# An attention and mixture-of-experts block: an own order for the last four batches, padding written during the steps, and expert rows turned by the transfer that loads them

## The chip, the cores and the metric

The kernel runs on one core of a Trainium2 chip. The metric is the time of one execution on the device, in microseconds (us). The core has a TensorE (PE, with its weight loads PEld), a VectorE (DVE), a ScalarE (ACT), a GpSimd (POOL), a SyncE (SP) that here only issues transfers, and 16 DMA engines that all queues share. TensorE runs at one of two clock levels, 1.2 and 2.4 GHz, shown as 0.5 and 1.0.

## The reference

Sixteen batches of 256 tokens of width 128 go through a block of two halves: causal linear attention with 16 heads, and a top-2 mixture of 8 experts. Each half is scaled, shifted and gated by vectors made from a condition `c`.

```python
h = layernorm(x) * (1 + ca) + sa
x = x + ga * attn(h)            # relu features, cumulative k v^T, num / den, out_w
h = layernorm(x) * (1 + cb) + sb
# ffn: 4096 tokens
u = h @ W_in.T;  h = rmsnorm(u, in_norm_w);  logits = h @ Wr.T
idx = top_k(logits + expert_bias, 2);  gates = softmax(logits[idx])
for e in range(8):
    oe = rmsnorm((silu(h @ Wg[e].T) * (h @ Wu[e].T)) @ Wd[e].T, enorm_w[e])
    out += gates[:, e] * oe
x = x + gb * (rmsnorm(out, out_norm_w) @ W_out.T)
```

## The kernel before

**Stage 1, the steps.** A batch passes through six stages of a software pipeline: `nrm` (first norm), `qkv`, `att` (running products of the attention), `prj` (division, output projection, second norm), `inp` (input projection of the experts, sum of squares) and `rte` (routing: best two experts, places, scatter of the rows). `pipelined` calls `step(nrm, qkv, att, prj, inp, rte)` on every engine with the batches s, s-1, ... s-5. Steps 0 to 7 are written out, steps 8 to 15 run in a loop, and steps 16 to 20 are written out again. In the last four of these, step 17 holds batch 15 in `att`, 14 in `prj`, 13 in `inp` and 12 in `rte`, and each later step has one stage fewer. Within a step every engine has one fixed order, written for a full step.

Routing of a batch b: ACT writes the high fp16 half of each row into `rows` (L595, L598); DVE then makes logits (L898), scores (L904), the low fp16 half (L952), the best two (L912, L919), their one-hot (L925); PE turns these into ranks (L1458 to L1464); DVE makes the places `pos` (L931, L947) and the counts (L938). POOL waits for `pos` and sends four indirect transfers of 128 rows of 516 B each (L524) into `hbuf` ("dispatched"), a DRAM buffer with a region of 4352 rows for each expert.

**Between the stages.** When batch 15 is counted, DVE makes `tail` (L1113, L1114), the end of each expert's rows, and SP and ACT write one padding tile of 256 rows (129 KB) behind each of the eight ends (L414, L717). DVE then makes the table of tiles (L1117 to L1136), the gates' logit differences (L1138 to L1143), and the low half of the down weights (L1148); ACT makes the high half (L703; chunks 0 to 2 in steps 18 to 20). SP waits for all scatters, all padding and the table before it loads the first tile.

**Stage 2, the experts.** 39 tiles of 256 rows, in turns of four. For each, SP loads 256 rows into one of four `slots` (L429), PE transposes them in four 128x128 blocks into PSUM (`transpose_rows`, L1504), DVE copies them to `hT3`, of which there are two (`put_hT`, L1167), and copies the places of the rows (`put_places`, L1173). PE then does gate and up (L1518 to L1520, 24 matmuls of 256 columns) and, for the tile before, down (L1533 to L1535, 24 of 128 columns). ACT and DVE do silu, product and split (L729, L735, L1180, L1185), ACT the squares, DVE the weighting (L1191), and POOL scatters the result (L543).

**Stage 3.** All rows are loaded again, the two of each token mixed, normed, projected and added.

## Time and profile before

| | us |
|---|---|
| median of 3 runs | 432.0 (431.47 to 436.98) |
| the profiled execution, whole | 440.27 |
| its span | 438.4 |
| busy in the span: PE / DVE / ACT / POOL | 366.1 / 338.8 / 290.9 / 249.9 |

The page of the profile shows the span in 40 slices of 10.96 us: each digit is the busy share of an engine in tenths. Three stages can be seen: the steps to about 181 us, the experts from about 228 us to 396 us, and the last part; between the first two stands the drain of the pipeline. The rows on which the prediction rests are in a section below. In a timeline a row is: start in us, duration in us, engine, line, operation, output<-input, shape, count, and in brackets the engine's idle time before it with what released it. A row that stands for several instructions gives the time from the first one's start to the last one's end.

### The profile page before, as it was taken

To read this page: it belongs to the slowest core of one execution; us is meant where nothing else is said; L and a number is where in the kernel's file an instruction comes from. 1 tells how busy PE (TensorE), PEld (TensorE's weight loads), DVE (VectorE), ACT (ScalarE), POOL (GpSimd) and SP (SyncE) were. 2 spreads that over 40 slices of the span, in tenths; PEclk is the share of its full clock that TensorE was granted. 3 is DMA by queue.
4 is the path that set the end of the run, shared out by engine and by line. 5 is a ranking of instruction groups with operands and counts; after the bars stand their busy time and mean duration, and the time that the engine had idled before them with its cause. 6 is when DMAs were issued, how large, how long until landed. Compare 5 with 4: busy or idle time off the path is not lost.

```text
span 438.4 us, 13203 instructions
## 1 busy us (share of the span) xinstructions
PE 366.1 (84%) x3906; PEld 321.1 (73%) x3907; DVE 338.8 (77%) x1113; ACT 290.9 (66%) x814; POOL 249.9 (57%) x221
## 2 busy tenths in 40 slices
PE   4799999979999999873129999999999999991464
PEld 3588878768888888762118999999999999981353
DVE  5077898869999998665599887878788788781586
ACT  4425768867888887534427776877768587773585
POOL 2964476668888888833532545456455554555341
PEclk9989999999999999985559999999999999998588
DMA  8994000000000000000141222122221222112933
GB/s 252 428 356 190 2 18 20 20 21 26 24 27 28 24 30 24 32 26 24 50 151 38 61 64 72 48 72 56 64 68 53 66 54 73 37 38 63 372 85 96
DMA packets 19107, 35.67 MB, mean 81 GB/s; under 512 B 3843, under 2 KB 14614, under 8 KB 18294
## 3 DMA queue, kind: packets, MB, share of 16 engines
q1 hardware_dynamic: 14262, 21.20, 15.4%
q0 software_dynamic: 4544, 9.39, 6.4%
q10 hardware_dynamic: 272, 4.72, 2.8%
q8 instruction: 15, 0.25, 0.2%
q14 instruction: 14, 0.11, 0.1%
HBM read 23.80 MB, written 13.47 MB: 85 GB/s over the span
## 4 chain that ended last, share of the span: by engine, by line
PE 56%; DVE 19%; issue 10%; DMA 7%; ACT 3%; POOL 3%; DVEq 1%; another core or an unknown queue 0%; ACTq 0%; SPq 0%; POOLq 0%
PE bank L1518 8%; PE bank L1520 8%; PE bank L1519 8%; PE bank L1335 6%; DVE prod L890 5%; PE bank L1533 4%; PE bank L1535 4%; PE bank L1534 4%; DMA gates_bc<-gate_rows 3%; PE bank L1504 2%; PE bank L1417 2%; DVE st L813 2%; PE bank L1444 1%; ACT junk L782 1%; DVE x_all L1085 1%
## 5 line engine op out<-in xcount | busy, mean ns | idle before, releaser
L543 POOL DMA_INDIRECT expert_rows<-late,to_place x78 | 86.7, 1111 | 83.2 <-DVE late L1191 56.8
L524 POOL DMA_INDIRECT dispatched<-rows,pos x64 | 67.1, 1049 | 38.0 <-issue 19.1
L1518 PE MATMUL bank<-late,w_hi 128*128 128x256 f16 x312 | 85.8, 275 | 1.5 <-issue 0.6
L1519 PE MATMUL bank<-late,w_hi 128*128 128x256 f16 x312 | 85.6, 274 | 0.0
L1520 PE MATMUL bank<-late,w_lo 128*128 128x256 f16 x312 | 85.6, 274 | 0.0
L506 POOL TENSOR_TENSOR kv<-kv,v 128x1024 f32<-128x1024 f32 x32 | 67.6, 2132 | 21.6 <-ACT kv L643 14.8
L1335 PE MATMUL bank<-cst,kv 128*128 128x128 f32 x576 | 77.0, 286 | 1.2 <-POOL kv L506 1.0
L1335 PEld LDWEIGHTS bank<-cst,kv 128*128 128x128 f32 x576 | 72.0, 201 | 1.9 <-POOL kv L506 1.1
L1180 DVE SCALAR_TENSOR_TENSOR kv<-bank,uscale,kv 128x512 f32<-128x512 f32 x78 | 58.0, 746 | 19.2 <-ACT kv L729 13.9
L729 ACT ACTIVATE kv<-bank,descale 128x512 f32<-128x512 f32 x78 | 53.5, 687 | 27.6 <-PE bank L1520 26.8
L735 ACT ACTIVATE kv<-kv 128x512 f16<-128x512 f32 x78 | 49.2, 631 | 20.5 <-DVE kv L1180 18.6
L1185 DVE TENSOR_TENSOR kv<-kv 128x512 f16<-128x512 f32 x78 | 53.6, 688 | 6.9 <-issue 4.9
L1533 PE MATMUL bank<-late,kv 128*128 x312 | 54.3, 219 | 1.3 <-DVE kv L1185 1.3
L1534 PE MATMUL bank<-late,kv 128*128 x312 | 54.3, 219 | 0.0
L1535 PE MATMUL bank<-late,kv 128*128 x312 | 54.3, 219 | 0.0
L890 DVE TENSOR_TENSOR prod<-bank,qT 128x384 f32<-128x384 f32 x96 | 49.8, 544 | 0.5 <-issue 0.3
L1518 PEld LDWEIGHTS bank<-late,w_hi 128*128 x312 | 30.7, 98 | 6.9 <-issue 2.9
L1520 PEld LDWEIGHTS bank<-late,w_lo 128*128 x312 | 30.7, 99 | 3.8
L1519 PEld LDWEIGHTS bank<-late,w_hi 128*128 x312 | 30.8, 99 | 3.2
L585 ACT ACTIVATE xn<-x_all,nmr,rs 128x128 f32<-128x128 f32 (+1 forms) x64 | 28.0, 485 | 6.5 <-DVE nmr L830 5.7
L1533 PEld LDWEIGHTS bank<-late,kv 128*128 128x128 f16 x312 | 30.5, 98 | 1.9 <-issue 1.4
L1534 PEld LDWEIGHTS bank<-late,kv 128*128 128x128 f16 x312 | 30.5, 98 | 0.4
(212 smaller groups left out, 797.1 us busy)
## 6 DMA issues: line engine op xcount, KB each, us to landing
late<-dispatched SPq DMA_DIRECT2D x39, 129.0 KB
late<-wguT ACTq DMA_DIRECT2D x1, 4096.0 KB, 15.8
late<-expert_rows SPq DMA_DIRECT2D x1, 2064.0 KB, 11.2
gates_bc<-gate_rows SPq DMA_DIRECT2D x1, 2048.0 KB, 15.1
wd<-wdT SPq DMA_DIRECT2D x1, 2048.0 KB, 23.8
out<-kv SPq DMA_DIRECT2D x16, 128.0 KB, 1.8
expert_rows<-late,to_place POOLq DMA_INDIRECT x78
late<-expert_rows SPq DMA_DIRECT2D x1, 1032.0 KB, 6.8
```

Source lines behind the costliest of these rows:

```text
L506: nc.gpsimd.tensor_tensor(kvt[:, 0:HD, :, :], k_in, v_in.to_broadcast([P, HD, H, HD]), ALU.mult).then_inc(kv_done[t], 1)
L524: pool.indirect_dma_start(hbuf, bass.IndirectOffsetOnAxis(ap=pos[:, p, t * K + k:t * K + k + 1], axis=0), rows[:, p, t, k, :], None).then_ ...
L543: pool.indirect_dma_start(ybuf, bass.IndirectOffsetOnAxis(ap=to_place[:, s, r:r + 1], axis=0), yt[:, s, r, :], None).then_inc(y_scat[s], 16)
L890: nc.vector.tensor_tensor(prod[:, t, cc * THIRD * P:(cc + 1) * THIRD * P].rearrange("p (e i) -> p e i", i=P), cum, qT[:, p, t * P:(t + 1) ...
L1180: nc.vector.scalar_tensor_tensor(gu[:, h, :], U[h], uscale[:], sg[:, h, :], ALU.mult, ALU.mult).then_inc(gu_done, 1)
L1335: last = mm(CUM[cc][:, j * P:(j + 1) * P], kv[:, p, t, e * D:(e + 1) * D], tri, start=True, stop=True)
L1518: mm(o, w_hi[:, w], hi, start=True, stop=False)
L1519: mm(o, w_hi[:, w], lo, start=False, stop=False)
L1520: last = mm(o, w_lo[:, w], hi, start=False, stop=True)
L1533: mm(o, gu_hi[:, s % 2, h, g], wd_hi[:, w], start=(f == 0 and r == 0), stop=False)
L1534: mm(o, gu_lo[:, s % 2, h, g], wd_hi[:, w], start=False, stop=False)
L1535: last = mm(o, gu_hi[:, s % 2, h, g], wd_lo[:, w], start=False, stop=(f == FC - 1 and r == RB - 1))
```

## The change

It has three parts.

1. **Drain.** `pipelined` runs step 16 as before and then, in the place of steps 17 to 20, calls a function `drain(b12, b13, b14, b15)` on each engine, in which the same work of the last four batches stands in another order, cut into smaller functions. Odd batches use a second PSUM place for the input projection (`UL_ODD`, in the bank of k and v), ranks and the total get PSUM places of their own (`LAST_RANK`, `TOTAL`), and scores and one-hots read their constants from SBUF. ACT writes the high halves after the logits, not before. The scales of the down weights are made in 6 DVE instructions where there were 9, between batch 14 and batch 15 and no longer in step 17; all four chunks of L703's work come after batch 15.
2. **Padding.** SP writes padding over all rows of all eight regions during the steps: 17 transfers of 256 rows x 8 regions (1.06 MB each, in rows of 516 B), at most two in flight. `pos` of batch b waits until transfer b has landed, so a row is scattered only after it was padded. `tail` and the eight padding tiles at the end are gone.
3. **Expert rows.** `slots`, `transpose_rows`, `put_hT` and `put_places` are gone. SP loads each tile with two transfers that transpose (256 rows x 128 fp16 to 128 partitions x 256), high and low half, into one of four `hT3`, and loads the places with a third transfer of 256 single words of 4 B. A load for tile t waits for the up matmuls of tile t-4, and the places wait for the scatter that used the buffer before. The logit differences (`choose_gates`) move behind tile 2, and the gates' sigmoid behind the last tile.

```diff
-        SLOTS, HT3, YT = (E * FC * D + n for n in (0, 4 * RB * HW, 4 * RB * HW + 2 * R))
-        slots = in_late(SLOTS, 4 * RB * HW).bitcast(U32).rearrange("p (s r w) -> p s r w", s=4, r=RB)
-        slots16 = in_late(SLOTS, 4 * RB * HW).bitcast(F16).rearrange("p (s r w) -> p s r w", s=4, r=RB)
-        ident16 = sb("ident16", [P, P], F16)
-        hT3 = in_late(HT3, 2 * R).bitcast(F16).rearrange("p (s n) -> p s n", s=2)
+        HT3, YT = E * FC * D, E * FC * D + TURN * R
+        hT3 = in_late(HT3, TURN * R).bitcast(F16).rearrange("p (s h n) -> p s h n", s=TURN, h=2)
...
-        def pipelined(eng, step):
+        def pipelined(eng, step, drain):
 
 
 
@@ -377,8 +375,8 @@
             with eng.Fori((B - WN) // 2 + 1, B // 2 + 1) as m:
                 for r in range(2):
                     step(*((2 * m - 2 + r - g, (r - g) % 2, m + (r - g) // 2) for g in stages))
-            for s in range(B, B + 5):
-                step(*(at(s - g) for g in stages))
+            step(*(at(B - g) for g in stages))
+            drain(*(at(B - 4 + g) for g in range(4)))
...
-            sp.wait_ge(tail_done, 1)
-            tail_regs = [sp.alloc_register(f"tail{e}") for e in range(E // 2)]
-            sp.load(tail_regs, tail[0:1, 0:E // 2])
-            for e in range(E // 2):
-                row = sp.snap(tail_regs[e], min_val=0, max_val=E * REGION - R)
-                sp.dma_start(hbuf[bass.ds(row, R), :], filler[e * R:(e + 1) * R, :]).then_inc(filled, 16)
+            sp.wait_ge(x_rest, 48)
+            sp.wait_ge(moe_ld, 32)
+            regions = hbuf[0:E * REGION, :].rearrange("(e r) w -> r e w", e=E)
+            padding = filler[0:E * R, :].rearrange("(e r) w -> r e w", e=E)
+            for s in range(REGION // R):
+                if s >= 2:
+                    sp.wait_ge(padded[s % 2], 16 * (s // 2))
+                sp.dma_start(regions[s * R:(s + 1) * R], padding).then_inc(padded[s % 2], 16)
...
+            def load_rows(t, s, i):
+                row = sp.snap(row_regs[s], min_val=0, max_val=HROWS - R)
+                if again_turn(i):
+                    sp.wait_ge(u3_ps, 2 * t - 6)
+                for half in range(2):
+                    sp.dma_start(hT3[:, s, half], hbuf16[bass.ds(row, R), half * D:(half + 1) * D],
+                                 transpose=True).then_inc(slot_ld[s], 16)
+
+            def load_places(s, i, reg):
+                row = sp.snap(reg, min_val=0, max_val=HROWS - R)
+                if again_turn(i):
+                    sp.wait_ge(y_scat[s], 16 * RB * i)
+                sp.dma_start(to_place[:, s].unsqueeze(2), hbuf[bass.ds(row, R), D:HW].rearrange(
+                    "(r p) w -> p r w", p=P), allow_slow_non_contiguous=True).then_inc(place_ld[s], 16)
 
             def load_tiles(i, tiles=TURN):
+                if again_turn(i):
+                    for s in range(2):
+                        sp.reg_mov(past_regs[s], row_regs[s + 2])
                 sp.load(row_regs, tile_row[0:1, bass.ds(TURN * i, TURN)])
                 for s in range(tiles):
-                    row = sp.snap(row_regs[s], min_val=0, max_val=HROWS - R)
-                    if again_turn(i):
-                        sp.wait_ge(place_done, TURN * i + s - 3)
-                    sp.dma_start(slots[:, s], hbuf[bass.ds(row, R), :].rearrange("(p j) w -> p j w", j=RB)).then_inc(
-                        slot_ld[s], 16)
+                    load_rows(TURN * i + s, s, i)
+                    if s >= 2:
+                        load_places(s - 2, i, row_regs[s - 2])
+                    elif again_turn(i):
+                        load_places(s + 2, i - 1, past_regs[s])
 
             load_tiles(0)
-            with sp.Fori(1, TURNS - 1) as i:
+            load_tiles(1)
...
+                act.wait_ge(lr_done, b + 1)
+                rows_high(b, p, n, UL_ODD if p else UL)
...
+            for c in range(DN):
                 projection_high(c)
-
-
-            act.wait_ge(tail_done, 1)
-            tail_regs = [act.alloc_register(f"act_tail{e}") for e in range(E // 2)]
-            act.load(tail_regs, tail[0:1, E // 2:E])
-            for e in range(E // 2, E):
-                row = act.snap(tail_regs[e - E // 2], min_val=0, max_val=E * REGION - R)
-                act.dma_start(hbuf[bass.ds(row, R), :], filler[e * R:(e + 1) * R, :]).then_inc(filled, 16)
...
                 dve.wait_ge(ohs_done, b + 1)
+                dve.wait_ge(padded[p], 16 * n)
...
+            def choice(b, p, n):
+                ul = UL_ODD if p else UL
+                dve.wait_ge(rms_done, b + 1)
+                nc.vector.reciprocal(rrs[:, p, :], rms[:, p, :]).then_inc(rrs_done, 1)
+                dve.wait_ge(rrs_done, b + 1)
+                logits(b, p, ul if b > B - 4 else UL)
+                scores(b, p, ebias[:])
+
...
+            def drain(b12, b13, b14, b15):
+                choice(*b12)
+                best_two(*b12)
+                denominators(*b14)
+                running_products(b15, 0)
+                rows_low(*b12)
+                quotients(*b14)
+                slots_of(*b12)
+                running_products(b15, 1)
+                count_chosen(*b12[0:2])
+                add_attention(*b14)
+                choice(*b13)
+                second_inverse(*b14)
+                second_shift(*b14)
+                denominators(*b15)
+                best_two(*b13)
+                rows_low(*b13)
+                slots_of(*b13)
+                quotients(*b15)
+                count_chosen(*b13[0:2])
+                add_attention(*b15)
+                choice(*b14)
+                second_inverse(*b15)
+                second_shift(*b15)
+                best_two(*b14)
+                rows_low(*b14)
+                slots_of(*b14)
+                count_chosen(*b14[0:2])
+                projection_scales()
+                choice(*b15)
+                best_two(*b15)
+                rows_low(*b15)
+                slots_of(*b15)
+                count_chosen(*b15[0:2])
...
-            def put_hT(t, s, i):
-                dve.wait_ge(slotT_ps, t + 1)
-                if s >= 2 or again_turn(i):
-                    dve.wait_ge(u3_ps, 2 * t - 2)
-                nc.vector.tensor_copy(hT3[:, s % 2, :], T[s % 2][:].bitcast(F16)[:, 0:2 * R]).then_inc(hT3_done, 1)
...
+                if h and again_turn(i):
+                    dve.wait_ge(y_scat[s], 16 * RB * i)
...
+                dve.wait_ge(place_ld[s], 16 * (i + 1))
...
+                    if first and s == 2:
+                        choose_gates()
...
+            def drain(b12, b13, b14, b15):
+                running_state(b15, 0, False)
+                pe.wait_ge(k_done, B)
+                pe.wait_ge(wsums_done, 2)
+                mm(KV[:, 0:2], ones, wsums[:], start=True, stop=True).then_inc(wnorm_ps, 1)
+                spread(*b14)
+                turn(*b13)
+                running_state(b15, 1, False, range(1))
+                ranks(*b12)
+                running_state(b15, 1, False, range(1, 3))
+                head_sums(b15, 0)
+                project(*b14)
+                into_experts(*b13)
+                head_sums(b15, 1)
+                spread(*b15)
+                ranks(*b13)
+                turn(*b14)
+                into_experts(*b14)
+                project(*b15)
+                ranks(*b14)
+                turn(*b15)
+                into_experts(*b15)
+                ranks(*b15)
...
-            def transpose_rows(t, s, i):
-                pe.wait_ge(slot_ld[s], 16 * (i + 1))
-                if s >= 2 or again_turn(i):
-                    pe.wait_ge(hT3_done, t - 1)
-                o = T[s % 2][:].bitcast(F16)
-                for half in range(2):
-                    for r in range(RB):
-                        last = nc.tensor.transpose(o[:, half * R + r * P:half * R + (r + 1) * P],
-                                                   slots16[:, s, r, half * D:(half + 1) * D], ident16[:])
-                last.then_inc(slotT_ps, 1)
-
             def gate_up(t, s, i, e, h, part):
                 if h == 0 and part == 0:
-                    pe.wait_ge(hT3_done, t + 1)
-                hi, lo = hT3[:, s % 2, 0:R], hT3[:, s % 2, R:2 * R]
+                    pe.wait_ge(slot_ld[s], 32 * (i + 1))
+                hi, lo = hT3[:, s, 0], hT3[:, s, 1]
```

**PE, from the last third of batch 15's first running state on** (`bank<-cst,kv`: running state; `bank<-cst,rden`: the denominators' transposes; `bank<-cst,xn`: transposes of the second norm; `bank<-gates_bc,attnT`: output projection; `bank<-small,h2T`: input projection; the rows of `region` and `oh_all`: ranks). Before:

```order
L1335 MATMUL bank<-cst,kv 128x128 x9
L1458 MATMUL bank<-region,ones 128x16
L1474 MATMUL bank<-small,h2T 128x136 x2
L1358 MATMUL bank<-prod,cst 32x128 x8
...
L1381 MATMUL bank<-cst,xn 128x128 x2
L1399 MATMUL bank<-cst,rden 128x128 x2
L1441 MATMUL bank<-bo_ga,oneb 128x256
L1444 MATMUL bank<-gates_bc,attnT 128x128 x2
L1458 MATMUL bank<-region,ones 128x16
```

Of the change, the same place:

```order
L1452 MATMUL bank<-cst,kv 128x128 x6
L1475 MATMUL bank<-prod,cst 32x128 x8
L1612 MATMUL bank<-bo_ga,oneb 128x256
L1615 MATMUL bank<-gates_bc,attnT 128x128 x2
L1627 MATMUL bank<-small,h2T 128x136 x2
L1470 MATMUL bank<-qT,s 32x128 x4
...
L1596 MATMUL bank<-cst,rden 128x128 x2
L1640 MATMUL bank<-region,ones 128x16
```

Batch 14's output projection now stands inside batch 15's head sums and no longer ahead of its running state, and the ranks of batch 12 stand one chunk into that running state.

**DVE, around the routing of batch 15** (`rrs`: the reciprocal that opens the choice; `rows`: low halves; `m`, `i`: best two; `ohs`, `pos`: places). Before:

```order
L1039 RECIPROCAL rrs<-rms 128x2
L898 TENSOR_TENSOR lr_all<-bank,rrs 128x16
L904 TENSOR_TENSOR score<-lr_all,bank 128x16
L952 SCALAR_TENSOR_TENSOR rows<-bank,rrs,rows 128x2x128 x2
L912 MAX m<-score 128x8 x2
L919 MAX_INDEX i<-m,score 128x8 x2
L925 TENSOR_TENSOR oh_all<-bank,i 128x32
L931 TENSOR_TENSOR ohs<-oh_all,bank 128x32
L947 TENSOR_REDUCE pos<-ohs 128x4
```

Of the change:

```order
L1028 TENSOR_SCALAR ydesc<-wpows 128x1
L1157 RECIPROCAL rrs<-rms 128x2
L948 TENSOR_TENSOR lr_all<-bank,rrs 128x16
L954 TENSOR_TENSOR score<-lr_all,ebias 128x16
L962 MAX m<-score 128x8 x2
L969 MAX_INDEX i<-m,score 128x8 x2
L975 TENSOR_TENSOR oh_all<-cst,i 128x32
L1003 SCALAR_TENSOR_TENSOR rows<-bank,rrs,rows 128x2x128 x2
L981 TENSOR_TENSOR ohs<-oh_all,bank 128x32
L998 TENSOR_REDUCE pos<-ohs 128x4
```

The low halves moved from ahead of the best two to behind the one-hot, so that PE can make the ranks beside them.

**PE, the start of the experts**, where batch 15's total is followed by the first tile. Before:

```order
L1484 MATMUL bank<-oh_all,ones 128x8
L1504 MATMUL bank<-ident,late 128x128 x8
L1493 TENSOR_LOAD tile_expert
L1494 ISA
L1518 ISA
```

Of the change:

```order
L1676 MATMUL bank<-oh_all,ones 128x8
L1685 TENSOR_LOAD tile_expert
L1686 ISA
L1699 ISA
L1699 MATMUL bank<-late,w_hi 128x256
```

The eight transposes of tiles 0 and 1 are gone, and so are the four in each later tile.

## Rows read from the trace of the kernel before

**Rows 1.** The page's 40 slices of 10.96 us: DMA share in tenths.

```profile
DMA  8994000000000000000141222122221222112933
```

**Rows 2.** Busy time by stretch; columns in the first line.

```profile
core 0: us, PE busy (x) PEld busy (x) DVE busy (x) ACT busy (x) POOL busy (x), PEclk, DMA share, GB/s
...
181.00:215.50 34.50, 17.14 (x154) 14.36 (x146) 18.88 (x100) 16.51 (x48) 15.60 (x17) 0.68 0.10 32
```

**Rows 3.** Timeline of PE, 180 to 230 us.

```profile
203.87 0.69 PE L1381 MATMUL bank<-cst,xn 128*128 128x128 f32 x2 [1.97 <-ACT xn L585]
...
214.65 0.19 PE L1458 MATMUL bank<-region,ones 1*128 1x16 bf16 x1 [5.35 <-issue]
...
228.57 0.39 PE L1518 MATMUL bank<-late,w_hi 128*128 128x256 f16 x1 [0.27 <-DVE late L1167]
```

**Rows 4.** Timeline of DVE, 180 to 230 us.

```profile
192.07 0.17 DVE L947 TENSOR_REDUCE pos<-ohs 128x4 uint32<-128x32 f32 x1
...
195.14 0.19 DVE L1034 TENSOR_SCALAR den<-bank 128x32 f32<-128x32 f32 x1 [1.06 <-PE bank L1364]
...
212.34 0.17 DVE L898 TENSOR_TENSOR lr_all<-bank,rrs 128x16 f32<-128x16 f32 x1 [1.70 <-ACT rows L598]
...
212.63 0.87 DVE L952 SCALAR_TENSOR_TENSOR rows<-bank,rrs,rows 128x256 f16<-128x256 f32 x2
...
215.33 0.19 DVE L947 TENSOR_REDUCE pos<-ohs 128x4 uint32<-128x32 f32 x1
```

**Rows 5.** Timeline of ACT, 180 to 230 us.

```profile
210.35 1.13 ACT L703 ACTIVATE late<-wd,wd_by 128x1024 f16<-128x1024 f32 x1
...
211.49 0.82 ACT L598 ACTIVATE rows<-bank,rrs 128x256 f16<-128x256 f32 x2
```

**Rows 6.** Groups, 181 to 216 us: count, busy us, mean ns, idle before.

```profile
L890 DVE TENSOR_TENSOR prod<-bank,qT 128x384 f32<-128x384 f32 x6 | 3.3, 547 | 0.3 <-PE bank L1335 0.2
L1474 PE MATMUL bank<-small,h2T 128*128 128x136 f32 x12 | 3.2, 413 | 0.0
```

**Rows 7.** Timeline of POOL: first scatter of batch 12, first and last of 15.

```profile
193.05 0.95 POOL L524 DMA_INDIRECT dispatched<-rows,pos  x1 [6.71 <-DVE pos L947]
...
216.32 0.96 POOL L524 DMA_INDIRECT dispatched<-rows,pos  x1 [2.13 <-DVE pos L947]
...
220.11 0.95 POOL L524 DMA_INDIRECT dispatched<-rows,pos  x1 [0.30 <-issue]
```

**Rows 8.** Timeline of SP's queue, 180 to 230 us: the padding issues.

```profile
217.26 2.68 SPq L414 DMA_DIRECT2D dispatched<-filler  x4
```

**Rows 9.** Waits of SP's queue: us in total, times, longest.

```profile
SPq L419 <- DMA dispatched<-filler: 4.3, 1, 4.3
```

**Rows 10.** Chain that ended last, 175 to 260 us: start, duration, what.

```profile
225.00 2.15 DMA late<-dispatched
...
249.54 0.22 PE bank L1504 x4
253.72 0.22 PE bank L1504 x4
```

**Rows 11.** Timeline of POOL at the experts' end: the last scatter.

```profile
401.11 0.96 POOL L543 DMA_INDIRECT expert_rows<-late,to_place  x1 [0.30 <-issue]
```

**Rows 12.** Timeline of SP's queue behind it.

```profile
403.53 1.76 SPq L442 DMA_DIRECT2D late<-expert_rows  x4
```

**Rows 13.** Groups of instructions, 250 to 390 us.

```profile
L1504 PE MATMUL bank<-ident,late 128*128 128x128 f16 x128 | 12.4, 219 | 0.0
```

**Rows 14.** SP's DMA queue, 420 to 437 us: packets, MB, share of 16 engines.

```profile
q1 hardware_dynamic: 3264, 1.57, 33.0%
```

**Rows 15.** The same queue, 250 to 390 us.

```profile
q1 hardware_dynamic: 4320, 3.96, 12.5%
```

**Rows 16.** Timeline of DVE, 48 to 182 us: `pos` of batches 0 and 11.

```profile
59.82 0.17 DVE L947 TENSOR_REDUCE pos<-ohs 128x4 uint32<-128x32 f32 x1
...
180.58 0.18 DVE L947 TENSOR_REDUCE pos<-ohs 128x4 uint32<-128x32 f32 x1
```

More of the change, by code:

```diff
@@ new lines, in squares @@
+            def squares(b, p, n, ul=UL):
+                act.wait_ge(u_ps, b + 1)
+                for t in range(NT):
+                    last = nc.scalar.activation(junk[:], ul[:, t, 0:D], ACT.Square, accum_out=ssq[:, p, t:t + 1])
+                    last.then_inc(ssq_done, 1)
+                    act.wait_ge(ssq_done, NT * b + t + 1)
+                nc.scalar.activation(rms[:, p, :], ssq[:, p, :], ACT.Sqrt, bias=eps_rms_h[:],
+                                     scale=1.0 / D / HSCALE ** 2).then_inc(rms_done, 1)
@@ L1483, in _ @@
+            pipelined(pe, step, drain)
             pe.wait_ge(count_done, B)
[L1484 removed]
+            mm(TOTAL, ones16[:], oh_all[:, B, NT * K, :], start=True, stop=True).then_inc(total_ps, 1)
             pe.wait_ge(table_done, 1)
```

335 lines of the change are left out of this document (207 added, 128 removed).

## The prediction, made before the changed kernel was run

> **What bounds the kernel now.** I read busy time by stretch first, then the chain of work that ended last, then the timelines of the drain, engine by engine. In the steps and in the expert stage PE has hardly a gap. Between them, from 181 to 215.5 us, no engine is full: PE works 17.1 of 34.5 us, half of that at the low clock level, and DVE 18.9 [rows 2]. This stretch is a chain of waits. PE stands 1.97 us before batch 15's second transposes, for the norm on ACT, and 5.35 us before batch 15's ranks [rows 3]. In those 5.35 us lie the squares, then 1.13 us of down-weight work on ACT ahead of the high halves (0.82 us), on which DVE waits 1.70 us [rows 5, 4], and then the low halves, 0.87 us, ahead of the best two [rows 4]. `pos` of batch 12 is written at 192.1 us and that of batch 15 at 215.33 [rows 4]. From there POOL scatters until 221.06 [rows 7]. SP would be free then but for the landing, and the wait it reports last is for the padding: four issues from 217.26 to 219.94 [rows 8], then 4.3 us until they have landed [rows 9], so 224.3. The first load takes 2.15 us from 225.00 [rows 10], and the first expert matmul starts at 228.57 [rows 3]. In the expert stage the four transposes of a tile start every 4.18 us and hold PE for 0.22 us [rows 10]; each is shown with 219 ns, since they overlap [rows 13].
>
> **The change part by part.**
>
> *Drain.* Durations below that have no group are estimates from the same instructions in the stretch of rows 2. DVE is free at 181.0. Choice and best two of batch 12 take 1.4 us, denominators of 14 0.6, three products of batch 15 3 x 0.65 (0.547 each [rows 6] and the small copy), one-hot and low halves 1.0 (0.87 [rows 4]), quotients 0.4, places 0.35: `pos` of 12 at 186.7, where it was at 192.1, 5.4 earlier. Three more products (1.5), counts (0.2) and batch 14's addition and statistics (1.3, behind PE's projection) end at about 189.9, as before. Batch 13's squares follow at 190.3. DVE then has choice 0.5, inverse and shift 0.5, denominators of 15 0.6, best two 0.8, one-hot and low 1.0, places 0.4, quotients 0.4: 194.5. PE's projection of 15 stands behind batch 14's input matmuls: 196.5. Addition and statistics 1.25: 197.75. Choice of 14 and shift of 15 1.0: 198.7. From there two branches. DVE routes batch 14 by 201.0. Batch 15 goes through the norm on ACT (until 200.0), transposes (200.9), the copy back (201.5), input matmuls of 1.1 us (four of 413 ns, overlapping [rows 6]; 202.6) and squares (203.8). The scales of the down weights, six instructions of about 0.2 us, fit on DVE before that. Batch 15's routing is then choice 0.5, best two 0.9, one-hot 0.2, and low halves 0.87 beside the ranks and the high halves, places 0.4: 2.8 us in place of about 5. `pos` of 15 would be at 206.6. Code that is written out once showed one wait with no partner in time, DVE's 1.06 us before `den` [rows 4], a microsecond behind PE's shown end; I allow one such: 207.7, **7.8 us earlier** than 215.5. POOL does not stop this: four scatters take 4.7 us (216.32 to 221.06 [rows 7]), and batch 14's would end at about 206.5. All of L703 comes behind, 4 x 1.13 = 4.5 us [rows 5], until about 210.5; DVE's table and low weights (4.8 and 4.9 us) end at about 218, just when the first tile may start.
>
> *Padding at the end.* With it gone, SP waits for the last scatter alone. At the experts' end that landing is quick: POOL ends at 402.07 and SP issues at 403.53, 1.46 us [rows 11, 12]. In the drain it was 224.3 - 221.06 = 3.3 us. **1.9 us earlier.** The tail's two DVE instructions (0.4 us) were hidden, as the table was ready at 221.2.
>
> *Padding in the steps.* 17 transfers of 2048 rows of 516 B, 128 rows for each of 16 engines. The queue that stores 512 B rows holds engines for 33.0% x 16 x 17 us / 3264 = 27.5 ns a packet [rows 14], the one that loads tiles 12.5% x 16 x 140 / 4320 = 65 ns [rows 15]. So one transfer takes 3.5 to 8.3 us; I take 5. DMA is idle after 38 us [rows 1], when they can start. Batch 0's `pos` is due at 59.8 and batch 11's at 180.6 [rows 16], 11 us apart. Even at 8.3 us transfer 0 lands at 46 and transfer 11 at 138. Nothing waits, cost 0. Nor does a scatter of a batch miss its buffer, with two steps to land. If that cover goes, it is rival B.
>
> *Expert rows.* The first tile: transposes, copy and their waits (227.15 to 228.57, 1.4 us) go; a second transfer and its issue (2.68 / 4 = 0.67 us [rows 8]) come. No row shows a transposing transfer. The lower bound is the plain load, 2.15 us [rows 10], the upper one two such loads one after the other, 4.3 us. I take about 2.9, nearer the plain one since it moves the same bytes, and gain **0** here (between +0.8 and -1.4). Tiles 2 to 38: the transposes leave PE, 37 x 0.22 = **8.1 us** [rows 10]. A load has three tile times (3 x 3.96 = 11.9 us) from the up matmuls of tile t-4 to its use, so its latency is hidden, and its rate matters only beyond 3.96 us a pair (rival A). DVE loses a copy and a place copy a tile, so it does not become the bound. SP's queue gets the word loads (256 packets of 4 B, 16 an engine): the places are used four tiles later. `choose_gates`, 1.6 us on DVE behind tile 2, fits in DVE's slack of the same size; the sigmoid falls in ACT's wait for the first rows. **+0.5 us** for DVE, which shares time with POOL's gate product (4.5 us from about 218) in tile 0.
>
> *The sum.* -7.8 - 1.9 + 0 - 8.1 + 0.5 = -17.3 us: span 438.4 to 421.1, whole execution 440.3 to 423. The profiled execution stands 8.3 us above the median; the stages that change are counted in microseconds in both. Median: 432.0 - 17.3 = 414.7, **415 us**.
>
> **A rule against it.** Rows 13 show a block on PE with 219 ns, of which 55 ns count. "VectorE: DVE Perf Modes" of the Trainium skill, in "The three transpose paths", gives 390 ns on TensorE and 1309 ns by DMA for 128x128, and its rules say to use TensorE if PSUM will do. No run yet shows the DMA's figure here. Hidden, it changes nothing in the sum; four blocks in a row would be 5.24 us a tile, an estimate from that page, and the stage 39 x 1.28 = 50 us longer, 465 us.
>
> **Rivals.**
>
> A. *The transposing loads become the bound.* Place: SP's queue and the DMA engines, in each tile. For it: a block is written across 128 partitions. Against: the plain load is a small share of the engines (12.5% [rows 15]). If a pair costs two plain loads in series, 4.30 us a tile, the stage loses 39 x 0.34 = 13.3 us of the gain: 428 us, within 2%. It is slower than before from 4.40 us a pair on (17.3 / 39 over 3.96), and by 2% from 4.62 on. 0.07 for 428. A pair of over 4.62, with twice as long a hold (some 5 us a pair, 455 us): 0.05; the page's rule is this case.
>
> B. *Padding holds `pos`: this one ends slower.* Transfer b must land before `pos` of b. With w us each it is 38 + 16w for batch 15, against 206.6: nothing below 10.5, slower than before beyond 11.6, by 2% beyond 12.2. At 12 us: 230, 23.4 late, 438 us. Against: both rows give under 8.3. For: reading and writing DRAM by rows of 516 B on both sides is not in the trace. "DMA: Bandwidth & Descriptors" of the Trainium skill, in "Issuing engines are not separate DMA queues", says that all these transfers interleave on the same 16 engines; the trace agrees as far as the landing of 3.3 against 1.46 us goes. 0.05.
>
> C. *The drain's new order gains little.* More waits like the 1.06 us, PE at the low level, ACT as the new chain: if `pos` of 15 gains 2 us only, 432.0 - 11.5 = 420.5 us. For it: batch 15's projection is only 3.5 us earlier in my chain. 0.10, of which 0.02 within 2%.
>
> D. *Small losses everywhere*, loads and padding slowing the steps and the start: 425 to 434 us, 0.03.
>
> **How the numbers follow.** Forecast 0.70 (408 to 421), C 0.10, A 0.07 and 0.05, B 0.05, D 0.03. Two per cent, 8.6 us, is about what a measurement here can tell from none. Faster by over 2% (under 423.4): 0.70 + 0.08 = 0.78. Within: 0.02 + 0.07 + 0.03 = 0.12. Slower: 0.10. The low end: the allowance not needed (-1.1), the start's 0.5 and 0.8, and some 4 for a chain that is shorter than I read it: 408. The high end takes in C, D's half and A's first case: 428.
>
> **What would show it.** `pos` of batch 12 at about 187 and of 15 at 207 to 208; POOL's last scatter ending near 212.5; SP's first load under 2 us later; the first expert matmul near 219; tiles every 3.96 us; no PE wait on `slot_ld`; DMA over half busy from 38 to about 120 us and `pos` of 0 and 11 where they were. I am wrong if tiles come at over 4.2 us, if `pos` waits for padding in the steps, or if `pos` of 15 stays beyond 212.

## The result and the profile after

The changed kernel takes 462.5 us (median of 4 runs, 459.8 to 464.0), the kernel before 434.0 beside it (431.5 to 437.0). The ratio is 1.065, 95% interval 1.055 to 1.075: **slower by 6.5%**, where 415 us was forecast. The profiled execution has a span of 461.9 us, against 438.4.

The slices of the changed kernel's page (11.5 us each) answer to [rows 1]:

```profile
PE   4799599695985958949951499999999999993374
...
PEclk9999889898895996979975699999999999998579
DMA  8999999999999999992011133333333323311923
...
q1 hardware_dynamic: 76678, 38.65, 53.5%
```

DMA, idle in the steps before, is full until about 208 us, and beside it PE has gaps in every second or third slice, where it had hardly any. The timeline of DVE shows the same in `pos`, here of batches 11, 12 and 15, for [rows 16, 4]:

```profile
223.12 0.18 DVE L998 TENSOR_REDUCE pos<-ohs 128x4 uint32<-128x32 f32 x1
228.60 0.19 DVE L998 TENSOR_REDUCE pos<-ohs 128x4 uint32<-128x32 f32 x1
...
248.35 0.19 DVE L998 TENSOR_REDUCE pos<-ohs 128x4 uint32<-128x32 f32 x1
```

Batch 11's places come 42.5 us later than before. From there to batch 15's it is 25.2 us in place of 34.8 (215.3 - 180.6). So the steps lose, and the stretch behind them gains. The waits say on what (line waited for: us in total, times, longest):

```profile
ACT rows L619 <- DMA dispatched<-rows,pos: 36.7, 5, 9.1
...
SPq L412 <- DMA dispatched<-filler: 148.1, 15, 12.4
```

It is not `pos` that waits for padding. ACT, about to write a batch's rows into one of the two `rows` buffers, waits for the scatter of the batch before last out of that buffer. The chain of waits names one such landing, between POOL's scatters of a batch and ACT (start, us, what; POOL's row is the third scatter, and the landing's row starts with the fourth, at 127.32):

```profile
126.06 0.96 POOL dispatched L547
127.02 0.30 issue
127.32 15.33 DMA dispatched<-rows,pos
...
142.76 0.21 ACT rows L619
```

The fourth scatter is issued at 127.3 and lands 15.3 us later. The chain has five such landings, of 12.9 to 15.4 us. The other end of the change is as forecast, again from the chain:

```profile
253.32 2.28 DMA dispatched<-rows,pos
255.60 0.02 SPq L420
...
256.33 1.21 SPq L430
...
257.69 2.25 DMA late<-dispatched
259.93 0.13 issue
260.06 0.39 PE bank L1699
```

The last scatter is seen by SP 2.3 us after its issue. From SP's first transposing issue to the first matmul it is 3.7 us, against 3.6 before [rows 3, 10]. From the first expert matmul to the end of the span it is 461.9 - 260.1 = 201.8 us, against 438.4 - 228.6 = 209.8 [rows 3]. The three pieces make the span: 438.4 + 42.5 (steps) - 11.0 (from batch 11's `pos` to the first matmul) - 8.0 (experts and end) = 461.9.

### The profile page after: what moved, and what is told of

It reads as the page before. It is cut to its first block, busy times and chain, and to the rows that moved or that the text cites. A ratio compares the mean times of both kernels' runs of the same rounds, so it can differ in the third digit from the quotient of the medians.

```text
span 461.9 us, 12906 instructions
## 1 busy us (share of the span) xinstructions
PE 369.6 (80%) x3750; PEld 321.9 (70%) x3751; DVE 322.8 (70%) x1027; ACT 291.9 (63%) x814; POOL 245.5 (53%) x221
## 4 chain that ended last, share of the span: by engine, by line
PE 51%; DMA 22%; issue 8%; DVE 7%; POOL 6%; ACT 5%; SPq 0%; DVEq 0%; ACTq 0%; POOLq 0%
DMA dispatched<-rows,pos 16%; PE bank L1699 8%; PE bank L1701 7%; PE bank L1700 7%; PE bank L1452 5%; POOL dispatched L547 4%; PE bank L1714 4%; PE bank L1715 4%; PE bank L1716 4%; DMA gates_bc<-gate_rows 3%; PE bank L1530 3%; POOL kv L529 1%; DVE prod L941 1%; ACT junk L834 1%; DVE prod L1361 1%
## 5 line engine op out<-in xcount | busy, mean ns | idle before, releaser
L570 POOL DMA_INDIRECT expert_rows<-late,to_place x78 | 81.6, 1047 | 80.3 <-DVE late L1313 67.7
L1699 PE MATMUL bank<-late,w_hi 128*128 128x256 f16 x312 | 85.8, 275 | 12.7 <-DMA late<-dispatched 11.2
L782 ACT ACTIVATE kv<-kv 128x512 f16<-128x512 f32 x78 | 48.8, 626 | 16.5 <-DVE kv L1299 10.6
L1699 PEld LDWEIGHTS bank<-late,w_hi 128*128 x312 | 30.8, 99 | 17.7 <-issue 14.1
```

The source lines that it names most:

```text
L570: pool.indirect_dma_start(ybuf, bass.IndirectOffsetOnAxis(ap=to_place[:, s, r:r + 1], axis=0), yt[:, s, r, :], None).then_inc(y_scat[s], 16)
L1699: mm(o, w_hi[:, w], hi, start=True, stop=False)
```

## Theories

**Backlog.** A scatter lands only behind the padding that the DMA engines hold already. With two transfers of 1.06 MB in flight that is one to two times 10 us. The buffer it frees is needed earlier than that, so ACT stalls, and the steps with it. **Share.** Padding and scatters merely take turns on the engines, however much is queued. **Rival B** of the prediction: `pos` waits for its padding. And for the size of it: does the number of pieces (2048 of 516 B) or the bytes (1.06 MB) make a transfer take 10 us?

## Experiments

### Which part of the change costs: e1_tails, e2_pad_only, e4_loads_only

**e1_tails**: the changed kernel, padding at the end again.

```diff
-            for s in range(REGION // R):
-                if s >= 2:
-                    sp.wait_ge(padded[s % 2], 16 * (s // 2))
-                sp.dma_start(regions[s * R:(s + 1) * R], padding).then_inc(padded[s % 2], 16)
+            sp.wait_ge(tail_done, 1)
...
+            sp.load(tail_regs, tail[0:1, 0:E // 2])
+            for e in range(E // 2):
+                row = sp.snap(tail_regs[e], min_val=0, max_val=E * REGION - R)
+                sp.dma_start(hbuf[bass.ds(row, R), :], filler[e * R:(e + 1) * R, :]).then_inc(filled, 16)
...
-                dve.wait_ge(padded[p], 16 * n)
```

> The changed kernel with the padding written at the end again (four pieces on SP, four on ACT, as before), the new order of the last four batches and the transposing loads kept. If the steps lost their 42.5 us to the padding alone, POOL's scatters land 1 to 3 us after their end, ACT's waits for the rows buffers (36.7 us) go, pos of batch 11 is at about 181 us again, and the time is 462.5 - 42.5 + about 1.5 for the tail = 417 to 422 us. If part of the loss of the steps, or part of the gain of the last batches, hangs on something else in the change (the new code of the last batches, more instructions on the engines), it stays above 428 us.

Measured: 420.7 us, ratio 0.969 (0.961 to 0.977). ACT waits for no scatter any more, a scatter lands after 2.3 us (median; at most 3.7), and batch 11's `pos` is at 177.6 us. The steps' loss is the padding's alone.

**e2_pad_only**: the kernel before with the padding in the steps, and nothing else.

```diff
-            sp.wait_ge(tail_done, 1)
...
+            for s in range(REGION // R):
+                if s >= 2:
+                    sp.wait_ge(padded[s % 2], 16 * (s // 2))
+                sp.dma_start(regions[s * R:(s + 1) * R], padding).then_inc(padded[s % 2], 16)
...
+                dve.wait_ge(padded[p], 16 * n)
```

> The kernel before with one part alone: the 17 padding transfers during the steps and the wait of pos for them; no padding at the end. If the padding alone holds the steps, the time is 434.0 + 42.5 - 2 = about 474 us, with ACT's waits for rows buffers of some 37 us. If the loss needs the new order too, it is 430 to 440 us.

Measured: 473.9 us, ratio 1.090 (1.081 to 1.099). Its waits, and the landings on its chain:

```profile
ACT rows L600 <- DMA dispatched<-rows,pos: 34.6, 5, 8.3
```

```profile
96.23 13.85 DMA dispatched<-rows,pos
...
125.72 14.09 DMA dispatched<-rows,pos
...
154.65 14.19 DMA dispatched<-rows,pos
...
184.18 14.29 DMA dispatched<-rows,pos
```

The loss needs nothing of the rest of the change.

**e4_loads_only**: the kernel before with the transposing loads alone.

```diff
+                for half in range(2):
+                    sp.dma_start(hT3[:, s, half], hbuf16[bass.ds(row, R), half * D:(half + 1) * D],
+                                 transpose=True).then_inc(slot_ld[s], 16)
...
-                    sp.dma_start(slots[:, s], hbuf[bass.ds(row, R), :].rearrange("(p j) w -> p j w", j=RB)).then_inc(
-                        slot_ld[s], 16)
...
-            transpose_rows(0, 0, 0)
-            transpose_rows(1, 1, 0)
```

> The kernel before with one part alone: the transposing loads of the expert rows (with the gates chosen behind tile 2 and the place loads, as in the changed kernel); order of the last batches and padding at the end as before. The traces give 8.0 us less from the first expert matmul to the end for the changed kernel: 434 - 8 = 424 to 428 us, ratio 0.975 to 0.987; the new order of the last four batches then makes the rest of e1_tails' 13.6 us, some 6 us. If the gain of the expert stage hangs on the new order (down weights ready earlier), it is 430 us or more.

Measured: 426.5 us beside 433.7, ratio 0.983 (0.979 to 0.987): 7.2 us less, a gain beyond the noise, though its interval reaches to both sides of 2%. The new order of the last batches is then worth 426.5 - 420.7 = 5.8 us. From batch 11's `pos` to batch 15's it is 31.8 us in this kernel and 25.5 in e1_tails, 6.3 less. The 34.8 of the profiled execution of before, 3.0 more with the same order, belongs to an execution that stood 6 us above its median.

### Pieces or bytes: e5_long, e9_two_rows

**e5_long**: the changed kernel, the same 17 transfers at the same places, in pieces of 16 rows.

```diff
-            regions = hbuf[0:E * REGION, :].rearrange("(e r) w -> r e w", e=E)
-            padding = filler[0:E * R, :].rearrange("(e r) w -> r e w", e=E)
+            regions = hbuf[0:E * REGION, :].rearrange("(e s q i) w -> s q e (i w)", e=E, q=16, i=R // 16)
+            padding = filler[0:E * R, :].rearrange("(e q i) w -> q e (i w)", e=E, q=16)
...
```

> The changed kernel, with the same 17 transfers of 1.06 MB, at the same places, but in 128 pieces of 8256 B each instead of 2048 pieces of 516 B. If the number of packets fills the DMA engines (76.7 ns for each of 128 packets an engine), a transfer now takes about 4 us (the pieces of 4.1 KB of the padding of before took about 250 ns each), all 17 are through by 110 us, a scatter has at most some 4 us of padding ahead of it, and the time is 415 to 425 us. If the bytes limit it (1.06 MB read and 1.06 MB written in 10.2 us), nothing changes: about 462 us. If the wait of pos for the padding is what holds the steps, then 420 us too, but with that wait as the one that went.

Measured: **416.8 us, ratio 0.960** (0.952 to 0.968), faster by 4%. Its slices and its waits:

```profile
DMA  7999998899100000010123433332333233214733
```

```profile
ACT rows L619 <- DMA dispatched<-rows,pos: 2.3, 1, 2.3
...
SPq L412 <- DMA dispatched<-filler: 51.5, 15, 5.1
```

```profile
dispatched<-filler SPq DMA_DIRECT2D x17, 1032.0 KB, 7.8
```

The padding is through by 105 us. Each transfer lands 7.8 us after its issue with two in flight, so 3.9 us each. The same bytes that filled the engines for 170 us now take under 70: the bytes do not set the 10 us. One wait for a buffer is left, 2.3 us.

**e9_two_rows**: pieces of two rows, 1032 B.

```diff
...
+            regions = hbuf[0:E * REGION, :].rearrange("(e s q i) w -> s q e (i w)", e=E, q=R // 2, i=2)
+            padding = filler[0:E * R, :].rearrange("(e q i) w -> q e (i w)", e=E, q=R // 2)
...
```

> The changed kernel, with the padding in pieces of two rows: 1032 B, 64 for each engine and transfer, instead of 128 of 516 B. In the changed kernel a packet of 516 B takes 76.7 ns; in e5_long 8 packets of 8256 B an engine take 7.8 / 2 = 3.9 us, 490 ns each. If a packet has a fixed cost of some 50 ns and the bytes cost the rest, one of 1032 B takes about 110 ns and a transfer 7 us; a scatter lands after some 9 us, ACT's waits are some 5 to 15 us, and the time is 420 to 432 us. If the packet's number alone sets it: 77 ns, 4.9 us, 417 to 422 us. If the bytes set it until pieces are long: 10 us, 455 us or more.

Measured: 433.9 us, 426.0 to 437.5 over 4 runs, so whether it is faster or slower than before stays open. The trace is that of the slowest, 437.5. A transfer takes 12.3 / 2 = 6.15 us, 96 ns for each of an engine's 64 pieces; in the changed kernel it was 10.2 / 128 = 80 ns a piece of 516 B, in e5_long 3.9 / 8 = 490 ns a piece of 8256 B. A straight line through the two ends (53 ns a piece and 53 ns per 1000 B) gives 107 ns for 1032 B, 11 more than measured. So a piece has a fixed cost about as large as what 1000 B cost, and neither the number nor the bytes alone set the rate: the transfer came out between the first two cases of the expectation. Two landings on its chain take 12.1 and 10.9 us, longer than the 9 expected, and ACT waits 15.6 us. The median came out above both ranges; in the fastest run, which has no trace, the time lies within the first.

### Backlog or share: e7_halves, e8_quarters, e12_quarters_four, e6_one

**e7_halves**: each transfer cut into two (by experts), two in flight.

```diff
...
+            for j in range(REGION // R * 2):
+                s, e0 = j // 2, j % 2 * E // 2
+                if j >= 2:
+                    sp.wait_ge(padded[j % 2], 16 * (j // 2))
+                sp.dma_start(regions[s * R:(s + 1) * R, e0:e0 + E // 2], padding[:, e0:e0 + E // 2]).then_inc(
+                    padded[j % 2], 16)
...
```

> The changed kernel, with each padding transfer cut into two of half the size, still two in flight: the same packets of 516 B and the same bytes at the same rate, but 1.06 MB instead of 2.1 MB waiting in the DMA engines when a scatter comes. Backlog theory: a scatter lands behind what the engines hold already, so about 10 us or less after its issue instead of 14, most of ACT's 36.7 us of waits for rows buffers goes, and the time is 425 to 445 us; padding is still done by about 215 us. Share theory (padding and scatter only share the engines packet by packet, whatever waits): the scatters land as late as before and the time stays at 455 to 465 us.

Measured: 437.5 us, ratio 1.008 (1.003 to 1.012). The landings on its chain and its waits:

```profile
112.11 10.45 DMA dispatched<-rows,pos
...
138.22 10.36 DMA dispatched<-rows,pos
...
163.50 9.14 DMA dispatched<-rows,pos
```

```profile
ACT rows L621 <- DMA dispatched<-rows,pos: 22.8, 7, 6.8
```

Half the bytes in flight, and 4 us less for a scatter to land (10.1 us on average on the chain against 14.1), at the same rate (10.46 MB in the 100 us from 60 on, 10.35 in the changed kernel). By taking turns packet by packet the landing would not have moved.

**e8_quarters**: the same with four cuts, two in flight (against e7_halves).

```diff
-            for j in range(REGION // R * 2):
-                s, e0 = j // 2, j % 2 * E // 2
+            for j in range(REGION // R * 4):
+                s, e0 = j // 4, j % 4 * E // 4
...
```

> The changed kernel, with each padding transfer cut into four (68 transfers of 0.26 MB, 512 packets of 516 B), two in flight. In the chain of waits a scatter lands 13 to 15 us after its issue with 2.1 MB in flight (e2_pad_only and the changed kernel), 9 to 10.5 us with 1.06 MB (e7_halves), 2.3 us with none (e1_tails). Backlog theory: with 0.53 MB in flight 5 to 7 us, which two steps cover almost; ACT's waits for the rows buffers are under 8 us (36.7 and 22.8 us before), pos of batch 11 is at 183 us or earlier, and the time is 418 to 428 us. If the padding's own rate falls by the shorter pieces (fixed cost of each, over 2.6 us a piece), pos waits for it instead (rival B) and the time is 435 us or more. If only the packets' number counts: 437 us as in e7_halves.

Measured: 437.5 us, ratio 1.009 (1.006 to 1.013). Its scatters (min, median, max to landing), its waits, and batches 13 to 15 on DVE's timeline:

```profile
DMA to landing us min/median/max: 2.7/5.0/7.0
```

```profile
DVE pos L1001 <- DMA dispatched<-filler: 23.6, 4, 7.7
```

```profile
199.87 0.19 DVE L1001 TENSOR_REDUCE pos<-ohs 128x4 uint32<-128x32 f32 x1 [5.44 <-DMA dispatched<-filler]
211.22 0.19 DVE L1001 TENSOR_REDUCE pos<-ohs 128x4 uint32<-128x32 f32 x1 [5.61 <-DMA dispatched<-filler]
222.98 0.19 DVE L1001 TENSOR_REDUCE pos<-ohs 128x4 uint32<-128x32 f32 x1 [7.72 <-DMA dispatched<-filler]
```

ACT's waits for buffers are 2.6 us, and the steps run as before (batch 11's `pos` at 177.2). Instead the padding is slower, 9.25 MB in the same 100 us, 11.4 us a transfer, and the last four batches wait for it: rival B has come. The engines are shown half idle (DMA 5 tenths), which the next run qualifies.

**e12_quarters_four**: e8_quarters with four of its transfers in flight.

```diff
-                if j >= 2:
-                    sp.wait_ge(padded[j % 2], 16 * (j // 2))
+                if j >= 4:
+                    sp.wait_ge(padded[j % 4], 16 * (j // 4))
...
```

> e8_quarters with four of the quarter transfers in flight instead of two: the same pieces, but 1.06 MB in flight as in e7_halves. In e8_quarters (0.53 MB in flight) a scatter landed after 5.0 us (median), ACT never waited for a rows buffer, and 1.06 MB of padding took 11.3 us, so that pos waited 23.6 us for it. Backlog theory: the bytes in flight count, not the number of transfers, so scatters land after 9 to 10.5 us as in e7_halves, ACT's waits are 15 to 25 us again, 1.06 MB takes 10.2 us, and the time is 432 to 440 us. If e8_quarters' rate was held only by its two short transfers (its packets are shown with 39 ns), 1.06 MB now takes 5 to 7 us, padding is through by 150 us and the time is 418 to 428 us.

Measured: 437.5 us, ratio 1.007 (1.003 to 1.012).

```profile
ACT rows L620 <- DMA dispatched<-rows,pos: 25.2, 10, 3.7
```

The landings on its chain are 8.9 to 10.6 us, those of e7_halves: bytes in flight count, not the number of transfers. The rate rises to 11.54 MB in the 100 us, 9.2 us a transfer where 10.2 was expected, and no further. So two short transfers in flight did not fill the engines, but four bring only a quarter more, not twice as much: pieces of 516 B do not go at 39 ns each, which e8_quarters' packets (44.9% of the engines' time for 18483) seemed to promise. The shown duration of a packet moves with what is in flight, so it is no price; the rate at which bytes land is.

**e6_one**: whole transfers, one in flight.

```diff
-                if s >= 2:
-                    sp.wait_ge(padded[s % 2], 16 * (s // 2))
+                if s >= 1:
+                    sp.wait_ge(padded[(s - 1) % 2], 16 * ((s + 1) // 2))
```

> The changed kernel, with one padding transfer of 1.06 MB in flight instead of two (the next is issued when the last has landed). Backlog theory: a scatter has at most 1.06 MB ahead of it, so 10 us or less, and ACT's waits for the rows buffers fall from 36.7 us to under 23 us; but a transfer then takes about 12 us (10.2 and about 2 to issue and land), the one that batch b needs lands at 38 + 12 (b + 1) us, batch 11's at 182, batch 15's at 230, and pos of batch 15 waits for it: some 15 us of waits of pos for the padding, 435 to 450 us in all. Theory that the wait for padding never binds: no such wait, 420 to 437 us.

Measured: 452.5 us, ratio 1.044 (1.036 to 1.052), a little above what was expected.

```profile
ACT rows L619 <- DMA dispatched<-rows,pos: 28.6, 11, 4.7
DVE pos L998 <- issue: 10.1, 2, 7.4
```

Both mechanisms at once. A transfer takes 10.8 to 12.7 us on the chain. `pos` of batches 14 and 15 comes at 216.1 and 227.3 us, after waits of 2.7 and 7.4 us whose releaser the view leaves at "issue"; the padding for batch 14 landed at 215.98. ACT's waits are shorter each (4.7 at most), but there are 11, 28.6 us in all, where I had expected under 23. Their ends show what a scatter waits for. Padding transfers land at 95.51, 107.25 and 118.47 us, and ACT, released by a scatter, starts at 96.20, 107.76 and 118.98; in nine of its ten waits between 84 and 192 us it starts 0.25 to 0.7 us after such a landing. A scatter lands with the end of the transfer that was ahead of it, so the steps run at the padding's pace (batch 11's `pos` at 194.7 us, 17 later than in e1_tails), and that costs more than in e7_halves with the same 1.06 MB in flight.

### The transposing loads: e10_blocks

**e10_blocks**: e5_long, with each tile loaded by four transposes of 128x128.

```diff
...
+                late_row = row + P
                 for half in range(2):
-                    sp.dma_start(hT3[:, s, half], hbuf16[bass.ds(row, R), half * D:(half + 1) * D],
-                                 transpose=True).then_inc(slot_ld[s], 16)
+                    for r, first in enumerate((row, late_row)):
+                        sp.dma_start(hT3[:, s, half, r * P:(r + 1) * P],
+                                     hbuf16[bass.ds(first, P), half * D:(half + 1) * D],
+                                     transpose=True).then_inc(slot_ld[s], 16)
...
```

> On e5_long, the transposing loads of a tile are cut into four of 128x128 instead of two of 256x128: the same bytes and the same layout. In the changed kernel SP's queue is held by 2.4 to 3.1 us for the two issues of a tile and 0.4 to 1.3 us for the place load, some 3.3 of 3.96 us. If an issue costs about 1.2 us whatever its size, SP needs 5.2 us or more a tile, becomes the bound of the expert stage, PE waits for slot loads and the time is 416.8 + 39 x 1.3 = 465 us or more. If the issue costs by its size, nothing changes: 415 to 420 us.

Measured: 496.5 us in a single run (465 us or more was expected). SP's queue, and below it that of the changed kernel:

```profile
299.50 4.92 SPq L432 DMA_TRANSPOSE late<-dispatched  x4
304.69 0.37 SPq L440 DMA_DIRECT2D to_place<-dispatched  x1
306.07 4.93 SPq L432 DMA_TRANSPOSE late<-dispatched  x4
```

```profile
341.03 0.37 SPq L437 DMA_DIRECT2D to_place<-dispatched  x1
341.64 2.41 SPq L430 DMA_TRANSPOSE late<-dispatched  x2
```

A transposing issue holds SP for 1.2 us, of 256 rows or of 128. Four and the place load make tiles of 5.8 us, and 6.6 at the start of each turn of four (the rows above): four tiles take 24.07 us (282.00 to 306.07), 6.0 each, and PE waits for the loads (45.0 us from 260 to 420 us). Over 39 tiles that is 39 x (6.0 - 3.96) = 80 us, the 79.7 by which this kernel is slower than e5_long. So rival A is real, on SP's queue and not in the DMA engines, which are 21% busy from 260 to 420 us. Two issues a tile, 6.0 - 2 x 1.23 = 3.6 us, stay some 0.4 us inside the 3.96 us of a tile.

### A version faster than both: e11_long_one

**e5_again** and **e11_long_one** ran side by side. The first is e5_long once more, the second has e6_one's edit on it, one transfer in flight.

> e5_long once more, with more rounds, beside e11_long_one on the same chip: 415 to 418 us, ratio 0.953 to 0.967.

> e5_long with one padding transfer in flight instead of two (pieces of 8256 B). Its one wait of ACT for a rows buffer (2.3 us, behind a scatter that took 8.2 us to land) should go, since at most 1.06 MB (3.9 us) is ahead of a scatter: landing at most 6.5 us; a transfer takes about 6 us, so the one for batch b lands at 38 + 6 (b + 1), long before its pos. Backlog theory: 413 to 417 us, 0 to 2 us under e5_again. If a transfer takes over 10 us so, pos of the later batches waits for it: over 420 us.

Measured: 416.8 us, ratio 0.961 (0.958 to 0.964), and 416.4 us, ratio 0.960 (0.957 to 0.963).

```profile
dispatched<-filler SPq DMA_DIRECT2D x17, 1032.0 KB, 5.5
```

In e11_long_one ACT waits for no scatter, as expected. The two cannot be told apart in time: e5_long's last wait was worth next to nothing.

## The padding in one table

In flight is what SP lets run at once; landing is that of the scatters on the chain (in e8_quarters, the median of all; in e1_tails likewise); per transfer is 1.06 MB over the rate, or the landings. The traces are one run each.

| kernel | piece | in flight | per transfer | scatter lands after | ACT waits | time |
|---|---|---|---|---|---|---|
| e1_tails | none in the steps | 0 | - | 2.3 us | 0 | 420.7 |
| e11_long_one | 8256 B | 1.06 MB | 5.5 us | - | 0 | 416.4 |
| e5_long | 8256 B | 2.11 MB | 3.9 us | 8.2 us (once) | 2.3 | 416.8 |
| e9_two_rows | 1032 B | 2.11 MB | 6.2 us | 10.9 and 12.1 us | 15.6 | 433.9 (426.0 to 437.5) |
| e8_quarters | 516 B | 0.53 MB | 11.4 us | 5.0 us | 2.6 | 437.5 |
| e7_halves | 516 B | 1.06 MB | 10.1 us | 8.8 to 12.5 us | 22.8 | 437.5 |
| e12_quarters_four | 516 B | 1.06 MB | 9.2 us | 8.9 to 10.6 us | 25.2 | 437.5 |
| e6_one | 516 B | 1.06 MB | 10.8 to 12.7 us | 9.0 us (once, batch 15) | 28.6 | 452.5 |
| changed kernel | 516 B | 2.11 MB | 10.2 us | 12.9 to 15.4 us | 36.7 | 462.5 |
| e2_pad_only | 516 B | 2.11 MB | 9.7 us | 11.6 to 14.3 us | 34.6 | 473.9 |

## Why the prediction was wrong

The step that failed is *Padding in the steps*, "Nothing waits, cost 0. Nor does a scatter of a batch miss its buffer, with two steps to land." It failed in three places.

**The time to land is 7 us, not two steps.** ACT writes batch b+2's high halves well ahead of that batch's `pos`. In e1_tails POOL issues a batch's fourth scatter at 110.58, and ACT writes into its buffer at 117.65:

```profile
110.58 0.96 POOL L545 DMA_INDIRECT dispatched<-rows,pos  x1 [0.30 <-issue]
```

```profile
117.65 0.21 ACT L617 ACTIVATE rows<-place_sb 128x4 uint32 x1 [1.01 <-DVE rrs L1091]
```

That is 7.1 us, of which the landing took 2.3. In the changed kernel the landing less the wait behind it leaves 15.33 - 9.06 = 6.3 us likewise. The trace of before has the same distance (112.8 to 120.0 us); I had counted steps between batches instead of reading the two rows.

**A scatter beside the padding is not a scatter alone.** I priced when the padding would be done, and not what its being in flight does to others. The prediction quoted that all transfers share the 16 engines, and used it for the padding's landing only. With 2.11 MB in flight a landing goes from 2.3 to 13 to 15 us. Less 6.3 of slack, that is a stall of 6 to 9 us, five times over: 36.7 us, of the 42.5 us that the steps lost. PE's granted clock is lower beside the gaps too, 0.88 from 38 to 206 us where e5_long shows 0.95; whether that makes the other 5.8 us is not shown. All of it goes with the padding (e1_tails).

**A row of 516 B between DRAM and DRAM costs 80 ns, not 27 to 65.** The upper bound, 65 ns, came from a queue that kept the engines 12.5% busy [rows 15]. I took 5 us for a transfer; it was 10.2. Even that is under rival B's threshold of 10.5, and so `pos` never waited for padding in the changed kernel. In e8_quarters at 11.4 and e6_one at some 12 us it did: the rival's formula, 38 + 16w, gives 220 us for batch 15's `pos` at 11.4, and e8_quarters shows 223.0; at 12 it gives 230, and e6_one shows 227.3. The rival had the right culprit and the wrong waiter, and 0.05 was too little for what 18 MB more on the engines (17 x 1.06) can hold up.

The rest of the sum held, by the runs with the fault taken out:

- *Drain*, 7.8 us forecast: 5.8 by the medians of e4_loads_only and e1_tails, 6.3 by their traces. `pos` of batches 12 to 15 was forecast at 186.7, 194.1 (194.5 less batch 15's quotients), 201.0 and 206.6 or 207.7; in the changed kernel, less the 42.5 us, it is at 186.1, 193.0, 199.9 and 205.8. The order was read right, though one term was summed low (batch 15's last three products at 1.5 us, where three times the 0.65 of the first three are 1.95). The base was not quite: the one execution of before took 3 us more for this stretch than e4_loads_only does with the same order, so a forecast in its microseconds promised too much.
- *Padding at the end*, 1.9 us: e1_tails and e5_long differ by 3.9 us in the median, and by 3.1 in the span. The chain shows 4.31 us of landing before SP's next step in e1_tails and 2.41 in e5_long, which is the 1.9 (the prediction's own rows, 3.3 - 1.46, make 1.8); `pos` of batch 15 comes 1.8 us earlier too, which I can't assign.
- *First tile*, 0: 3.7 against 3.6 us.
- *Tiles*, 8.1 less 0.5: 7.2 us by e4_loads_only. Rival A did not come, but the margin is some 0.4 us a tile and lies in SP's issues, which I had priced at 0.67 us each [rows 8] and not at 1.2.

Together: 434.0 - 17.3 = 416.7 us, and e5_long takes 416.8. The parts held, to 2 us each; that the total fits to 0.1 is luck, since the drain gave 2.0 less than forecast and the end of the padding 2.0 more. The forecast was the time of a kernel whose padding is in long pieces.

On *the rule against it*: "VectorE: DVE Perf Modes" of the Trainium skill ("The three transpose paths") gives 1309 ns for a 128x128 block by DMA. e10_blocks shows 1.23 us of SP's queue for such a block, close to it, but the changed kernel 1.2 us for a load of twice the size; so the page's figure times four blocks, 5.24 us a tile, did not come, since a tile needs two issues. That the 465 us of this rule stand near the measured 462.5 is chance: the expert stage, which it would have made 50 us longer, became 8.0 us shorter.

On the backlog, "DMA: Bandwidth & Descriptors" of the Trainium skill says in "Queues, rings and completion order" two things. An engine takes its queues in turn, packet by packet (a packet of that page holds several descriptors); by that alone a scatter would wait for a few packets only, and e7_halves contradicts it as an account of the landing. And the write that reports a transfer done lands only after all earlier writes of that engine, across its queues; the traces agree with that so far as landings grow with the bytes in flight. It is not the report alone that is late. In e1_tails all 128 DMA packets of a batch's four scatters (queue q0, 32 a scatter) have begun 2.0 us after the fourth one's issue at 110.58. In the changed kernel POOL issues four from 153.88 to 158.41, and the queue shows 57 packets until then and 11 more until 164.67: some 60 had not begun 6.3 us after the fourth issue. Why the engines take them up so late is not shown. The padding's 17 transfers and the scatters go to one DRAM buffer, and that this plays no part was not tried either.

## What to carry to other kernels

A transfer that "has time" still has a price: what it has in flight is added to the landing of every short transfer beside it. So find in the trace, for each of those, the distance from its issue to the instruction that needs its buffer, and compare that with the bytes in flight divided by their measured rate. Move filler data in pieces as long as the layout allows, and with little in flight. And take a stretch's length from more than one execution, or at least say how far the profiled one stands from the median.

## What the runs showed of the hardware that I had not expected

- DRAM to DRAM, 1.06 MB in 2048 pieces of 516 B takes 10.2 us on 16 engines, in 1024 of 1032 B 6.15 us, in 128 of 8256 B 3.9 us.
- A scatter of POOL lands 2.3 us after its issue with the engines free, 5.0 us with 0.53 MB of 516 B pieces in flight, about 10 with 1.06 MB and 12 to 15 with 2.11 MB (the last two from the chains, which name the landings that were waited for).
- Two short transfers in flight (0.26 MB each) take 11.4 us for 1.06 MB, with the engines shown 45% busy; four bring 9.2, at 96%.
- With one transfer of 1.06 MB in flight (e6_one), a scatter released ACT 0.25 to 0.7 us after a padding transfer landed, nine times out of ten.
- Beside the padding, some 60 of the 128 packets of four scatters had not begun 6.3 us after the last issue; on free engines all had after 2.0 us.
- The shown duration of a 516 B packet moves between 39 ns (44.9% busy, 9.25 MB in 100 us) and 77 ns (97.0%, 10.35 MB), at rates of bytes 12% apart.
- A transposing load of fp16 holds SP's queue 1.2 us, whether it has 256 or 128 rows of 128.
